# Attention kernel: weighted sums issued in half-width pieces, and the first semaphores raised earlier

## What is computed

```
xn = _layernorm(x)
q = split(xn @ q_w.T + q_b) / sqrt(16); k = split(xn @ k_w.T + k_b); v = split(xn @ v_w.T + v_b)
attn = softmax(einsum('bhqd,bhkd->bhqk', q, k))
ctx = einsum('bhqk,bhkd->bhqd', attn, v)
out = x + (ctx @ out_w.T + out_b) + ffn_fp8(xn)
```

## Time and profile before

| | us |
|---|---|
| median of three runs | 1905.96 |
| lowest, highest | 1904.66, 1906.21 |
| the profiled execution, its own time | 1905.45 |
| span of its trace, first to last instruction | 1903.6 |
| ScalarE busy | 1774.4 |
| TensorE busy | 1656.3 |
| VectorE busy | 1544.7 |

### The profile page before, as it was taken

How to read it: one execution, slowest core, us unless ns; L and a number is a source line. 1 busy time by engine, 2 the same in 40 slices (tenths; PEclk the granted TensorE clock), 3 DMA queues, 4 the chain that set the end, 5 groups by cost and what they waited for, 6 DMA issues and landing times.

```text
span 1903.6 us, 75615 instructions
## 1 busy us (share of the span) xinstructions
PE 1656.3 (87%) x33482; PEld 564.1 (30%) x33482; DVE 1544.7 (81%) x1974; ACT 1774.4 (93%) x1961; POOL 29.9 (2%) x48
## 2 busy tenths in 40 slices
PE   6978888888888888888888888888888888888888
PEld 4622222222222222222222222222222222222227
DVE  7667888878787887878787887878788887878787
ACT  2359999999999999999999999999999999999991
POOL 0000000000000000000000000000000000000000
PEclk9989999999999999999999999999999999999999
DMA  6640000000010000000010000001000000000002
GB/s 179 205 144 8 23 9 15 21 15 21 7 29 7 16 15 15 21 15 21 7 29 7 11 21 15 21 7 28 7 23 9 15 20 16 21 7 29 7 15 98
DMA packets 62334, 57.12 MB, mean 30 GB/s; under 512 B 20608, under 2 KB 52608, under 8 KB 62016
## 3 DMA queue, kind: packets, MB, share of 16 engines
q1 hardware_dynamic: 62016, 52.36, 9.4%
HBM read 34.74 MB, written 17.30 MB: 27 GB/s over the span
## 4 chain that ended last, share of the span: by engine, by line
ACT 51%; issue 30%; PE 14%; SPq 2%; DVE 1%; ACTq 1%; DMA 0%; DVEq 0%
ACT probs L688 51%; PE banks L1328 5%; PE banks L1297 3%; PE banks L1179 2%; PE banks L1420 1%; PE banks L1190 1%; ACTq L687 1%; DVE o_junk L975 1%; DVE o_sb L974 1%; PE banks L1404 0%; SPq L368 0%; PE banks L1412 0%; PE banks L1163 0%; SPq L371 0%; DMA k_parts<-probs 0%
## 5 line engine op out<-in xcount | busy, mean ns | idle before, releaser
L688 ACT ACTIVATE probs<-banks 128x1024 f32<-128x1024 f32 x1888 | 1731.1, 1193 | 6.7 <-DMA k_parts<-probs 6.2
L1328 PE MATMUL banks<-probs,v_st 64*32 64x512 f32 x15104 | 1004.2, 590 | 2.4
L1297 PE MATMUL banks<-q_st,k_st 50*32 50x512 f16 x16384 | 792.9, 381 | 217.4 <-ACT probs L688 214.2
L1297 PEld LDWEIGHTS banks<-q_st,k_st 50*32 50x32 f16 x16384 | 232.6, 89 | 1151.5 <-ACT probs L688 1093.4
L1008 DVE SCALAR_TENSOR_TENSOR horner<-horner,bits 128x1024 f32<-128x1024 f32 x320 | 393.2, 1229 | 11.0
L1328 PEld LDWEIGHTS banks<-probs,v_st 64*32 64x32 f32 x15104 | 272.0, 106 | 67.4 <-DVE o_junk L975 11.7
L995 DVE TENSOR_SCALAR bits<-banks 128x1024 int32<-128x1024 f32 x160 | 195.9, 1224 | 96.5 <-PE banks L1297 96.5
L1008 DVE SCALAR_TENSOR_TENSOR horner<-bits 128x1024 f32<-128x1024 f32 x160 | 196.1, 1226 | 5.5
L1013 DVE SCALAR_TENSOR_TENSOR d_probs<-horner,powers 128x1024 f32<-128x1024 f32 x160 | 196.0, 1225 | 5.5
L974 DVE COPY o_sb<-banks 128x512 f32<-128x512 f32 x32 | 22.1, 692 | 131.1 <-PE banks L1328 131.1
L1004 DVE TENSOR_SCALAR bits<-bits 128x1024 int32<-128x1024 int32 x160 | 111.1, 695 | 5.5
(11 more groups left out here) (112 smaller groups left out, 465.8 us busy)
## 6 DMA issues: line engine op xcount, KB each, us to landing
q_st<-q_parts SPq DMA_DIRECT2D x204, 32.0 KB, 1.8
k_st<-k_parts SPq DMA_DIRECT2D x102, 64.0 KB, 2.2
k_st<-k_parts SPq DMA_DIRECT2D x102, 60.0 KB, 2.1
q_st<-neg_row SPq DMA_DIRECT2D x264, 1.0 KB, 1.7
xnT_copy<-probs SPq DMA_DIRECT2D x8, 512.0 KB, 3.1
probs<-xnT_copy SPq DMA_DIRECT2D x8, 512.0 KB, 4.3
w_f<-xnT_copy SPq DMA_DIRECT2D x16, 256.0 KB, 2.7
out_dram<-horner SPq DMA_DIRECT2D x16, 256.0 KB, 2.1
```

The lines of the kernel that those rows point to most:

```text
L688: act.activation(probs[:, at:at + WIDE * CHUNK].rearrange("p (t c) -> p t c", t=WIDE), banks[:, bank:bank + WIDE, :], ACT.Exp, bias=EXP_SHIFT,
L1297: last = pe.matmul(banks[cols, bank + g, :], k_st[rows, keys], blocks[rows, j], start=True, stop=True, tile_position=(g * GROUP, t * VCOLS))
L1328: last = pe.matmul(banks[VCOLS * qb:VCOLS * (qb + 1), 6 + half, cols], v_st[keys, kt, :], src[keys, g * CHUNK:(g + 1) * CHUNK][:, cols], s ...
```

## The change

There are three edits.

**1. Sums in pieces.** The first sum of a unit stays whole. Each of the other 31 becomes two pieces of 256 columns each, with the same weights loaded again for the second, and `pv_done` is raised after the second. One piece stands after each place, two where more than three pieces are ready (`BACKLOG` 3) and after the last place. After the place that follows one of VectorE's (the maxima's place counts among these: 10, 20, 24, 34, 44, 54) stands none.

**2. Maxima.** The piece of place 19 stands between the two halves of the maxima.

**3. Start.** SyncE adds the 23 start values right after the load of tokens 8 to 15 (in units of 128), ahead of the loads of v's weights and of all that follows. ScalarE makes its first copy ahead of scaling the q and k weights.

```
-        SUMS_FROM, BACKLOG, D_DELAY = 6, 2, 11
+        SUMS_FROM, BACKLOG, D_DELAY = 6, 3, 11
...
-                left = list(range(KT))
+                busy = [p + 1 for p in self.takes]
+                left = [(0, None)] + [(at, piece) for at in range(1, KT) for piece in range(2)]
...
-                    now = [at for at in left if ready[self.sum_rows[at]] <= p]
-                    take = now[0:1] if (p - SUMS_FROM) % 2 == 0 or len(now) > BACKLOG or p > self.places else []
-                    self.sums_at[p] = [(at, None) for at in take]
+                    now = [piece for piece in left if ready[self.sum_rows[piece[0]]] <= p]
+                    take = now[0:2] if len(now) > BACKLOG or p > self.places else now[0:1]
+                    if p == SUMS_FROM:
+                        take = now[0:1]
+                    if p in busy:
+                        take = []
+                    self.sums_at[p] = take
...
             load_x(8, 16, x_in[1])
-            load_w("v")
-            for i in range(2):
-                sp.dma_start(bv_sb[:, i, :], bv.partition_broadcast(P)).then_inc(v_bias_in, 16)
-            load_x(16, 24, x_in[1])
-            load_x(24, 32, x_in[1])
-            load_w("f")
-            load_w("o")
-            for t, b in ((bo_sb, bo), (bf_sb, bf)):
-                for i in range(2):
-                    sp.dma_start(t[:, i, :], b.partition_broadcast(P)).then_inc(of_bias_in, 16)
             for s, n in ((lo_done, LO_0), (v_done, V_0),
...
                 sp.sem_inc(c.d_taken, D_0)
+            load_w("v")
+            for i in range(2):
+                sp.dma_start(bv_sb[:, i, :], bv.partition_broadcast(P)).then_inc(v_bias_in, 16)
+            load_x(16, 24, x_in[1])
+            load_x(24, 32, x_in[1])
+            load_w("f")
+            load_w("o")
+            for t, b in ((bo_sb, bo), (bf_sb, bf)):
+                for i in range(2):
+                    sp.dma_start(t[:, i, :], b.partition_broadcast(P)).then_inc(of_bias_in, 16)
...
             root(0)
+            copy_turned(0, 0, SAVED_0)
             act.wait_ge(scale_ready, 1)
             for i, n in enumerate("qk"):
...
-            copy_turned(0, 0, SAVED_0)
...
-                            scores(h, n)
-                            sums_of(h, n)
+                            if c.order[n % c.places] is None:
+                                maximum_scores(h, n, 0)
+                                sums_of(h, n)
+                                maximum_scores(h, n, 1)
+                            else:
+                                scores(h, n)
+                                sums_of(h, n)
```

More of the change, by code:

```diff
@@ L1212, in attend, with max_part @@
             def attend(c):
[L1213 to L1225, removed]
+                def max_part(bank, v, g, done, halves):
+                    if g:
+                        pe.wait_ge(c.max_half, halves)
+                    rows = slice(g * GROUP, g * GROUP + KROWS)
+                    for j in range(QB // GROUPS):
+                        at, to = v * UG + j * CHUNK, VCOLS * (QB // GROUPS * g + j)
+                        last = pe.matmul(banks[to:to + SAMPLED, bank, :], k_st[rows, 0:SAMPLED], q_st[rows, at:at + CHUNK],
+                                         start=True, stop=True, tile_position=(g * GROUP, to))
+                    last.then_inc(done if g else c.max_half, 1)
                 def all_max_jobs(h, v):
@@ L1276, in scores @@
                     buffer_free(h, n)
[L1277 to L1282, removed]
                     kt, j = c.order[p]
@@ L1299, in scores, with maximum_scores @@
                     last.then_inc(c.st_done, 1)
+                def maximum_scores(h, n, g):
+                    u = n // c.places
+                    v, nxt = 1 - u, h + u
+                    if not g:
+                        buffer_free(h, n)
+                        pe.wait_ge(c.q_in[v], nxt * LOADS + LOADS)
+                        pe.wait_ge(c.k_first, nxt * LOADS + LOADS)
+                    max_part(WIDE * ((h * c.head_places + n) % BUFS), v, g, c.st_done, h * UNITS + (u + 2))
                 def weighted_sum(h, u, at, piece):
@@ L1383, in attend @@
                             pe.wait_ge(v_done, V_0 + 2 * NCH)
-                            max_part(6, 0, 1).then_inc(c.misc_full, 1)
+                            for g in range(GROUPS):
+                                max_part(6, 0, g, c.misc_full, 1)
                     pe.wait_ge(c.misc_free, 1)
```

## The result

| | before | after |
|---|---|---|
| median of five runs, us | 1905.96 | 1914.3 |
| lowest, highest | 1904.66, 1906.21 | 1913.32, 1914.93 |
| span of the profiled execution | 1903.6 | 1912.4 |

The change makes the kernel slower: ratio 1.0044, 95% interval 1.0031 to 1.0057. The forecast was 1915 with a range of 1908 to 1926.

A forecast was written before the change was run, and what follows sets the result against it. ScalarE's 1888 exponentials at 0.917 us each were taken as the bound. Units +11.0, first unit +0.3, start -1.95 and end -0.1 make +9.25 on 1905.45, 1914.7, called 1915; forecast 1911 to 1920 (67%), range 1908 to 1926 (about 80%).

The forecast's parts named there:

- ScalarE's rate by the ends, floor 1.02: ScalarE's exponentials: each ends at its start + 1.02 or the end before + 0.917 us, whichever is later.
- A piece at 0.433: Sums on TensorE: a piece of 256 columns takes half of a whole sum's 0.86 us and a little, 0.433.
- The dearer piece of 0.455: Rival on TensorE's sums: about 60 cycles of overhead per matmul, 1920 in all; dearer pieces 12% for 1920 to 1928.
- Pieces of 0.54: Rival's extreme on TensorE's sums: a burst of weight loads shows in each piece, total near 1955; 4% above 1928.
- one place only: Rival in each unit: place 57 fits by a hair or 24 loses half, 1907 to 1911; chance 5%.
- Places 20 to 24: Edit 1 in each unit: pieces make the scores of 24 late, so ScalarE loses 0.285 us.
- E + 2.45: Start of place 24's scores on TensorE, 2.45 us after E, the end of place 18's exponential.
- Places 54 to 57: Edit 1 in each unit: pieces ahead of the scores of 57 make its exponential end 0.06 us late.
- Late starts that go bring nothing: Places where sums were taken away: nothing comes back, since their late starts cost nothing before.
- The first unit: First unit, TensorE at 1.2 GHz for part: loss of 1.15 in place of 0.86 us, +0.3; range -0.9 to +0.5.
- The start: Edit 3: ScalarE's first copy no longer waits for SyncE, first projection at 18.95 not 20.92, -1.95 us; range -2.3 to 0.
- The end: After the last exponential: half a sum fewer ahead of its sum, -0.1 us; range -0.4 to +0.2.

The follow-up runs named there:

- light sums: Kernel before with every sum but a unit's first over 128 columns in place of 512: 1911.44 us, ratio 1.0030.
- sums alone: Changed kernel with edit 3 undone, leaving the sums in pieces and the split maxima: 1917.45 us, ratio 1.0063.
- moved sum: Kernel before, all sums whole, with the sum after the scores of place 20 moved behind those of 21: 1919.52 us, ratio 1.0076.
- five and seven sets: Kernel before with place 29's scores computed again, five or seven extra sets: 1906.72 us, ratio 1.0008, and 1920.54 us, ratio 1.0080.
- edit 3 alone: Kernel before with only the start edit (start values raised earlier, first copy ahead of the scaling): 1904.42 us, ratio 0.9996.
- no rule: Changed kernel without the rule that leaves places behind VectorE's without a piece: 1904.53 us, ratio 1.0001 to the kernel before.
- rule out at the maxima: Changed kernel in which place 20, behind the maxima, may have a piece, the other empty places kept: 1905.54 us, ratio 1.0005.
- warmed: Kernel before with edit 3 and six extra float32 matmuls on TensorE behind the first three scores: 1902.61 us, ratio 0.9987.
- raise alone: Kernel before with start values raised early but ScalarE's first copy still behind the scaling: 1903.76 us, ratio 0.9991.

## Why the prediction was right, step by step

The forecast of 1915 met 1914.3, and the main term, the units' +11.0, is right in mechanism and size. That the total is so near is partly luck in two smaller terms, the first unit and the start.

*ScalarE's rate by the ends, floor 1.02.* Right. In every kernel the exponentials that end late are 1.02 to 1.03 long, and the kernel that was to test the rate (light sums) has no shorter unit.

*A piece at 0.433.* Right. Two pieces hold TensorE from 410.78 to 411.65, one from 411.87 to 412.30: 0.435 and 0.43. The dearer piece of 0.455, which the prediction worked out from a fixed overhead in each matmul, isn't there. Two prices of rivals were off, without effect on the forecast. Pieces of 0.54 would have given some 1946 and not 1955, since what place 22 or 56 loses is part of what 24 or 57 loses and isn't added to it. And with place 57 fitting, the time would have been 1912.8, outside the 1907 to 1911 of "one place only".

*Places 20 to 24.* Forecast 0.285, measured 0.28; scores of 24 forecast at E + 2.45, measured E + 2.44. *Places 54 to 57.* 0.06 and 0.06. Places 22, 36 and 56 were to fit, and do. Per unit 0.345 forecast, 0.33 measured; 11.0 us forecast, 10.6 measured.

*Late starts that go bring nothing.* Right: the kernel without the empty places has late starts at other places than the kernel before (20, 34, 36, 54 and 56 in place of 11, 21, 35, 45 and 55; both at 10) and the same 54.08.

*The first unit.* Forecast 0.3 more, measured 0.46 more. The losses are at places 7, 8 and 10, as forecast, but the third is 0.71 and not 0.5. By the table above some 0.3 of the difference is the pieces': sums alone loses 1.74 where kernels of whole sums with the same clock lose 1.43 and 1.44. So the term was right for the pieces. What it left out is that the clock's rise moves against the first exponential from one execution to the next, here from 8.0 to 8.4 us behind it; with the kernels of whole sums alone that is worth anything from 0.14 to 1.59. What sets that time wasn't measured.

*The start.* Forecast -1.95, in the profiled execution -2.32. That agreement is partly luck, and the term was too large by 0.7. First exponentials of the six profiled executions with the old start order (the kernel before, sums alone, moved sum, light sums, five and seven sets) lie between 121.3 and 123.2, mean 122.2; the six with the early raise (the change, edit 3 alone, no rule, rule out at the maxima, warmed, raise alone) between 120.4 and 122.0, mean 120.9. So the gain is nearer 1.25 than 1.95, and one pair of executions may show anything from a loss of 0.7 to a gain of 2.8. The step that was mis-sized: I took both ends of the 1.95 from one trace. The first projection, at 20.92 there, is the latest of the six with the old order (19.94 to 20.92, mean 20.60), for ScalarE's copy then starts anywhere from 18.74 to 19.70 behind SyncE's raise. With the early raise nothing hides the end of the transposes any more, 16.94 in that trace and anything from 16.54 to 17.76 in these six: in the five with edit 3 the first projection starts 2.2 behind it. Its mean over the six is 19.36, not 18.95. The two together are the 0.7.

*The end.* Forecast -0.1, measured +0.15. The thirteen traces spread over 48.80 to 50.09 from the last exponential to the end, so a term of this size can't be told from chance.

## What to carry to other kernels

Where one engine is saturated and, as ScalarE here, takes up its instructions before the last has ended, judge a change of order by the ends of its instructions and not by the starts; a late start is free until it passes the queue's slack, and then costs one for one. A rule that keeps work away from one place moves it to the next, so count what then stands between two hand-overs: here one sum one place later in each unit cost 14 us in 1905. A wait ended by a semaphore that another engine raises only once, at the end of a list of loads, is worth looking for at the start of a kernel. Where a term is smaller than the spread between executions, as the start and the first unit are here, one pair of traces doesn't give its size.

## What was not expected of the hardware

Less work on TensorE made the kernel slower. With a quarter of the columns in most sums, the granted clock fell from 0.997 to 0.678 on average, scores and the whole first sums ran at 1.2 GHz for part of the time, and ScalarE lost 0.08 to 0.33 us in all units but one that it doesn't lose beside the full sums: 6 us in all. The reverse worked too: 5.4 us of useless matmuls in a wait of the start went with a clock that stayed at 1.00 and a first unit without loss, where the other kernels of the table lost 0.14 to 1.74. What exactly makes the clock fall in the light kernel wasn't measured, nor was a kernel run in which TensorE has little to do at the full clock.
